# Gated delta stage on one Trainium2 core: fills of the update banks moved, last list through a key bank, norm written in its own order

## The chip, the cores and the metric

The kernel runs on one core of a Trainium2 chip. The metric is the device time of one execution in microseconds (us). The core's engines run their own instruction lists and wait for one another through semaphores: TensorE (PE in the profile, with its weight loads as PEld), VectorE (DVE), ScalarE (ACT), GpSimd (POOL) and SyncE (SP), which issues the DMAs.

## The reference

The program is four layers of attention and feed-forward, each followed by a residual sum and a normalization. The change touches the first one, a gated delta rule, in float32:

```python
q = _causal_dwconv_silu(x @ Wq.T, qcw, qcb)            # 16 heads of 64 channels, 4 taps
k = _causal_dwconv_silu(x @ Wk.T, kcw, kcb) * SCALE
v = _causal_dwconv_silu(x @ Wv.T, vcw, vcb)
a = jax.nn.sigmoid(x @ Wa.T + ba)
beta = jax.nn.sigmoid(x @ Wb.T + bb)

def step(S, inp):
    qt, kt, vt, at, bt = inp
    err = jnp.einsum('bhij,bhj->bhi', S, kt) - vt
    S = at[..., None] * S - bt[..., None, None] * (err[..., None] * kt[:, :, None, :])
    o = jnp.einsum('bhij,bhj->bhi', S, qt)
    return (S, o)

mu = o.mean(-1, keepdims=True)
var = ((o - mu) ** 2).mean(-1, keepdims=True)
o = (o - mu) / jnp.sqrt(var + EPS) * ln_w + ln_b
g = jax.nn.sigmoid(x @ Wg.T)
return (o * g) @ Wo.T
```

The kernel holds 4 sequences of 512 steps, so 4 x 16 heads = 64 states of 64 x 64.

## The kernel before

The stage is `delta_attention`. It takes the 512 steps in 16 passes of 32 (`NC`, index `n`); each pass has two halves of 16 steps (`e` = 0 and 1), and each half two quarters of 8 (`u`). Heads lie in pairs (`NP` = 32) on the 128 partitions.

DVE sets the pace. A half is: `begin` (transposes the start products out of PSUM, L2784), `steps` for the first quarter, the transposed list of values `W` (L2836), `middle` (decays the state `ST`, L2808, then takes what the first quarter gives to the second out of PSUM, L2810), `steps` for the second quarter, `W` again (L2838), and the end of the half: `end` transposes the outputs (L2862) and the next pass's decays and values (L2743, L2744); in the first half `norm` normalizes and gates the outputs of the pass before (L2867, L2870), in the second `gate_keys` transposes the products of keys for the next pass out of PSUM (L2732, L2736). Then `prepare` (L2749, L2752) and the next `begin`.

PE serves this chain. At the end of each half `boundary` updates the state: it turns `W` with 4 transposes (L2476), waits until ACT has copied them to `WT` (L2647, semaphore `wc`), adds 64 small products to the decayed state in four PSUM banks, one bank per row quarter `r` (L2466; `UPDATES` = banks 6, 7, 0, 1), and after ACT has copied each bank back to `ST` (L2659, `state`) makes the start products of the next half (L2442), which DVE's L2784 waits for. The decayed state comes into those banks by a product with the identity, 128 x 512, here called a fill (`kept`, L2447). Between these PE projects the next pass: decays, values, keys, queries (L2381, L2384), into banks 0 and 1 by turns, from where ACT evacuates them (L2593, `evac`). It also makes the products of keys (L2395, 64 of them, into banks 2 to 5), those of the later quarters (L2405), keys across (L2435), centring, gate and variance (L2498, L2502, L2509), the cross products for `middle` (L2416, L2428), and the output projection of the pass before (`out`, L2517).

The order of each engine's work is written out by hand in its `one_pass`. Which bank is free sets most of it. Before the change the lists of the second half were turned in bank 1:

```python
UPDATES = (6, 7, 0, 1)
TURNED = ((2, 3), (1, 1))
EARLY = (4, 3)
```

so in the first half all four banks were filled ahead of `W`, and in the second three; bank 1 was filled after the updates of the other three, and its 16 updates came after that.

Of the kernel before, what the change touches and what calls it, by code (L numbers as in the profile page):

```python
# [15 lines left out]
ALU = mybir.AluOpType  # L16
# [2219 lines left out]
def delta_attention(c):  # L2236
# [7 lines left out]
    M = 8  # L2244
# [4 lines left out]
    NP = B * M  # L2249
# [3 lines left out]
    I = 32  # L2253
    GR, GP = 4, NP // 4
    UPDATES = (6, 7, 0, 1)
    TURNED = ((2, 3), (1, 1))
    EARLY = (4, 3)
    ACROSS = (2, 3)
    BEGUN = 7
    GC = 2 * SB * CP + SB  # L2260
    names = ("loaded", "staged_k", "staged_q", "staged_v", "prepared", "beta_ps", "beta", "proj", "evac", "kq", "g", "gt", "kt", "ktc",
# [3 lines left out]
    s = {n: c.nc.alloc_semaphore(name="dl_" + n) for n in names}  # L2265
    with ExitStack() as ctx:
# [51 lines left out]
        PROJ = 8  # L2318
        K, QQ, V, A = range(4)
        ORDER = (A, A, V, V, K, K, QQ, QQ)  # L2320
        AV = 4
# [49 lines left out]
        def _(eng):  # L2371
            def project(m, first, last, fresh):
                for i in range(first, last):
                    if i - first >= 2 or not fresh:
                        eng.wait_ge(s["evac"], m * PROJ + i - 1)
                    w, half = ORDER[i], i % 2
                    for r in range(4 * half, 4 * half + 4):
                        out = ps[:, i % 2, (r % 4) * P:(r % 4 + 1) * P]
                        cols = slice(r * P, (r + 1) * P)
                        if w == A:  # L2380
                            mm = eng.matmul(out, Wa[:, cols], columns_of(c.X, m, PAD), start=True, stop=True)  # L2381
                        else:
                            for tap in range(TAPS):
                                mm = eng.matmul(out, taps[w][:, tap, cols], columns_of(c.X, m, tap),  # L2384
                                                start=tap == 0, stop=tap == TAPS - 1)
                    mm.then_inc(s["proj"], 1)

            def products_of_keys(m):
                eng.wait_ge(s["kq"], m + 1)
                eng.wait_ge(s["evac"], (m + 1) * PROJ)  # L2390
                eng.sem_inc(c.past, 1)
                for pair in range(NP):
                    for h in range(2):
                        rows, w = slice(DK * h, DK * h + DK), pair % 2
                        mm = eng.matmul(keys_ps[DK * (h ^ w):DK * (h ^ w) + DK, w, pair // 2, :], kkN[rows, pair, :, :].rearrange("p k t -> p (k t)"),  # L2395
                                        kqN[rows, pair, :, :].rearrange("p t k -> p (t k)"), start=True, stop=True)
                mm.then_inc(s["g"], 1)

            def later_products(m):
                for e in range(2):  # L2400
# [45 lines left out]
            def kept(r):  # L2446
                eng.matmul(ps[:, UPDATES[r], :], c.ident[:, :], quarters[:, r, :, :], start=True, stop=False)  # L2447

            def keep_early(n, e):
                eng.wait_ge(s["decayed"], 2 * n + e + 1)  # L2450
                for r in range(EARLY[e]):
                    kept(r)

            def boundary(n, e):
                j4 = 8 * n + 4 * e

                def next_start(r):
                    eng.wait_ge(s["state"], j4 + max(r + 1, 2 * e))
                    eng.sem_inc(c.past, 1)
                    start(1 - e, r)  # L2460

                def update(g, k, h, r):
                    rows, cols = slice(32 * r, 32 * r + 32), slice(DK * h, DK * h + DK)
                    at = (2 * g + k) * DK
                    last = (g, k, h) == (GR - 1, 1, 1)
                    mm = eng.matmul(ps[cols, UPDATES[r], at:at + DK], KT[rows, e, k, g, cols],  # L2466
                                    WT[rows, g, DK * (h ^ k):DK * (h ^ k) + DK], start=False, stop=(g, k) == (GR - 1, 1))
                    if last:
                        mm.then_inc(s["upd"], 1)

                early = EARLY[e]
                eng.wait_ge(s["w"], 4 * n + 2 * e + 2)
                eng.sem_inc(c.past, 1)
                for half in range(2):
                    for g in (2 * half, 2 * half + 1):
                        mm = eng.transpose(ps[:, TURNED[e][half], g * P:(g + 1) * P], W[:, g * GP:(g + 1) * GP, :], c.ident[:, :])  # L2476
                    mm.then_inc(s["t"], 1)
                eng.wait_ge(s["wc"], 6 * n + 3 * e + 3)
                eng.sem_inc(c.past, 1)
                for g, k, h, r in itertools.product(range(GR), range(2), range(2), range(early)):  # L2480
                    update(g, k, h, r)
                for r in range(early, GR):
                    kept(r)
                    for g, k, h in itertools.product(range(GR), range(2), range(2)):
                        update(g, k, h, r)
                for r in range(GR):
                    next_start(r)
                if e == 1:
                    eng.wait_ge(s["gt"], 2 * n + 3)
                    eng.sem_inc(c.past, 1)  # L2490
                    later_products(n + 1)
# [20 lines left out]
            def out(n):  # L2512
                eng.wait_ge(s["normed"], n + 1)
                eng.sem_inc(c.past, 1)
                Dv = Q[:, :].rearrange("p (m x) -> p m x", m=M)
                for m in range(M):
                    mm = eng.matmul(ps[:, 6, 0:P], Wo[:, m, :], Dv[:, m, :], start=m == 0, stop=m == M - 1)  # L2517
                mm.then_inc(s["wo"], 1)

            def one_pass(n, first):  # L2520
                keys_across(n)
                eng.wait_ge(s["ktc"], 5 * n + 1)
                if not first:
                    centre(n - 1)
                project(n + 1, 0, 2, True)
                eng.wait_ge(s["ktc"], 5 * n + 5)
                middle(n, 0)
                if not first:
                    variance(n - 1)
                project(n + 1, 2, AV, False)  # L2530
                eng.wait_ge(s["evac"], (n + 1) * PROJ + AV)
                if not first:
                    eng.wait_ge(s["log"], 2 * n - 1)
                keep_early(n, 0)
                boundary(n, 0)
                project(n + 1, AV, 6, True)
                if not first:
                    out(n - 1)
                project(n + 1, 6, 7, False)
                middle(n, 1)  # L2540
                project(n + 1, 7, PROJ, False)
                if not first:
                    eng.wait_ge(s["scaled"], n)
                    eng.wait_ge(s["wo_copied"], n)
                eng.wait_ge(s["evac"], (n + 1) * PROJ + 7)
                keep_early(n, 1)
                eng.wait_ge(s["begun"], BEGUN * (2 * n + 1) + 5)
                products_of_keys(n + 1)
                boundary(n, 1)
# [11 lines left out]
            project(0, 6, PROJ, False)  # L2561
            eng.wait_ge(s["staged_q"], 32 + 16 * len(late))
            products_of_keys(0)
            eng.wait_ge(s["gt"], 2)
            eng.sem_inc(c.past, 1)
            later_products(0)
# [160 lines left out]
        def _(eng):  # L2727
# [10 lines left out]
            def turn_values(m, e):  # L2738
                span = slice(e * CH, (e + 1) * CH)
                eng.wait_ge(s["evac"], m * PROJ + AV)  # L2740
                if 2 * m + e > 2:
                    eng.wait_ge(s["laid"], 4 * (2 * m + e - 2))
                eng.transpose(decays[:, :, :], aN[:, span, :]).then_inc(s["transposed"], 1)  # L2743
                eng.transpose(values[:, :, :], vN[:, span, :]).then_inc(s["transposed"], 1)  # L2744
# [112 lines left out]
                settled()  # L2857

            def end(n, e, first):
                if e == 0 and not first:  # L2860
                    eng.wait_ge(s["centred"], n)
                eng.transpose(O[:, e * CH:(e + 1) * CH, :], OT.rearrange("p i t -> p t i")).then_inc(s["o"], 1)  # L2862
                turn_values(n + 1, e)

            def norm(n):
                eng.wait_ge(s["log"], 2 * n + 2)
                eng.scalar_tensor_tensor(D[:, :], centred_ps, vec[:, LW:LW + 1], Q[:, :], ALU.mult, ALU.mult).then_inc(s["scaled"], 1)  # L2867
                eng.wait_ge(s["scaled"], n + 1)
                by_row = "p (x m) -> p x m"
                eng.scalar_tensor_tensor(Q[:, :].rearrange("p (m x) -> p x m", m=M), D[:, :].rearrange(by_row, m=M), vec[:, LB:LB + 1],  # L2870
                                         gate[:, :, :].rearrange("p t n -> p (t n)").rearrange(by_row, m=M), ALU.add, ALU.mult)\
                   .then_inc(s["normed"], 1)

            def residual(n):
# [207 lines left out]
```

## Time and profile before

| | |
|---|---|
| time, median of 3 runs | 2895.76 us (2886.55 to 2899.36) |
| the profiled execution | 2886.77 us, span 2885.0 us |
| PE busy | 2413.8 us (84%) |
| DVE busy | 2070.2 us (72%) |
| ACT busy | 1604.8 us (56%) |
| delta stage, about 60 to 1310 us: DVE busy | 1092.4 us |
| the same: PE busy | 1006.6 us |
| the same: mean granted clock of PE | 0.86 |

Times are microseconds from the start of the span. A row of the timeline gives start, duration, engine, line of the kernel, operation, tiles and count; in brackets stands the idle time before it and who ended it. A float32 product leaves two records on PE, a transpose one. The granted clock is 1.00 at 2.4 GHz and 0.50 at 1.2 GHz. A matmul's end is modelled, so where two groups stand back to back the difference of their starts is the better price.

### The profile page before, as it was taken

Reading aid. Unit: us, or ns where it says so; the run is one execution under the profiler, and the core shown is the slowest. Engines: PE = TensorE matmul, PEld = TensorE weight load, DVE = VectorE, ACT = ScalarE, POOL = GpSimd, SP = SyncE. Lnnn points to the kernel's source line nnn. Section 1 sums busy time; section 2 is a strip of 40 time slices with the busy share of each in tenths; the row PEclk is TensorE's granted clock in tenths of the full one; section 3 lists DMA queues with packets and bytes.
Section 4 is the critical chain, followed back from the end, with each engine's and each line's share of the span. In section 5 each row is a group of like instructions: output and inputs, shape, how many; then the busy total and the mean of one; then the engine's idle time right before and its main releaser. Section 6 shows DMA issues by size and latency. Waiting matters only on the chain. (4 is left out here: it accounts for less than half of the span.)

```text
span 2885.0 us, 63703 instructions
## 1 busy us (share of the span) xinstructions
PE 2413.8 (84%) x25649; PEld 1614.8 (56%) x25701; DVE 2070.2 (72%) x3811; ACT 1604.8 (56%) x4104; POOL 260.7 (9%) x278
## 2 busy tenths in 40 slices
PE   6788778887788787788994999999987877998687
PEld 5666667666666666664442666666542322332376
DVE  6888898888888888983113777788626766885365
ACT  3666666666666665665234777777631113776244
POOL 0000000000000000000011101100002432110422
PEclk9888898888888888987996999999998998999889
DMA  5111011111111110102006999999410003220422
GB/s 183 32 32 30 18 31 32 31 32 25 24 31 32 32 32 17 31 17 70 1 11 166 237 250 227 227 248 235 105 37 0 0 0 113 68 68 18 180 58 64
DMA packets 205725, 219.47 MB, mean 76 GB/s; under 512 B 32966, under 2 KB 191446, under 8 KB 199990
## 3 DMA queue, kind: packets, MB, share of 16 engines
q1 hardware_dynamic: 203033, 210.44, 28.0%
q0 software_dynamic: 2400, 4.95, 0.5%
q8 instruction: 206, 3.38, 0.5%
q14 instruction: 86, 0.70, 0.1%
HBM read 137.96 MB, written 79.79 MB: 75 GB/s over the span
## 5 line engine op out<-in xcount | busy, mean ns | idle before, releaser
L2850 DVE TENSOR_REDUCE dl_ZO<-dl_XP 128x64 f32<-128x128 f32 (+6 forms) x448 | 219.8, 491 | 15.4
L1990 ACT ACTIVATE da_AB<-ps 128x384 f32<-128x384 f32 x256 | 124.5, 490 | 139.1 <-PE ps L1851 135.4
L2845 DVE TENSOR_TENSOR dl_XP<-dl_ZO,dl_G 128x128 f32<-128x128 f32 (+5 forms) x384 | 177.1, 461 | 13.2
L2000 ACT ACTIVATE da_E<-ps,da_top 128x512 f32<-128x512 f32 x256 | 176.1, 688 | 17.6 <-DVE da_top L2146 17.2
L1470 DVE TENSOR_REDUCE ra_top<-ps 128x1 f32<-128x512 f32 x256 | 159.3, 681 | 36.0 <-PE ps L1236 22.8
L2143 DVE TENSOR_TENSOR ps<-ps,da_window 128x192 f32<-128x192 f32 (+1 forms) x256 | 101.3, 396 | 115.0 <-PE ps L1874 110.7
L2146 DVE TENSOR_REDUCE da_top<-ps 128x1 f32<-128x512 f32 x256 | 177.0, 691 | 8.8
L1881 PE MATMUL ps<-ident,da_E 128*128 128x128 f32 x1024 | 169.1, 288 | 1.3 <-ACT da_E L2000 1.3
L1370 ACT ACTIVATE ra_PT<-ps 128x512 f32<-128x512 f32 x256 | 135.9, 602 | 61.1 <-PE ps L1267 59.2
L2447 PE MATMUL ps<-dl_ST,ident 128*128 128x512 f32 x256 | 136.1, 667 | 21.5 <-ACT dl_vN L2593 21.5
L1601 POOL MEMSET da_K<- 32x4096 f32 x2 | 7.0, 3506 | 1502.4 <-POOLq L195 1502.3
L2647 ACT ACTIVATE dl_WT<-ps 128x256 f32<-128x256 f32 x64 | 21.1, 381 | 210.9 <-PE ps L2476 210.9
L2384 PEld LDWEIGHTS ps<-X,dl_taps_v 128*128 128x128 f32 x1088 | 128.8, 197 | 14.0 <-issue 9.9
L1881 PEld LDWEIGHTS ps<-ident,da_E 128*128 128x128 f32 x1024 | 108.5, 141 | 50.1 <-issue 39.6
L2384 PE MATMUL ps<-X,dl_taps_v 128*128 128x128 f32 x1088 | 128.5, 279 | 3.7 <-DVE dl_taps_v L2906 3.2
L2384 PE MATMUL ps<-X,dl_taps_k 128*128 128x128 f32 x1088 | 130.3, 280 | 0.2 <-issue 0.2
L2384 PE MATMUL ps<-X,dl_taps_q 128*128 128x128 f32 x1088 | 129.5, 276 | 0.0
L2384 PEld LDWEIGHTS ps<-X,dl_taps_k 128*128 128x128 f32 x1088 | 126.8, 196 | 1.2 <-issue 0.5
L2675 ACT ACTIVATE dl_FB<-dl_F,dl_beta_now 128x32 f32<-128x32 f32 x512 | 126.6, 350 | 0.0
L2384 PEld LDWEIGHTS ps<-X,dl_taps_q 128*128 128x128 f32 x1088 | 125.1, 192 | 1.1
L2833 DVE TENSOR_TENSOR dl_ZO<-dl_ZO,dl_aT 128x64 f32<-128x64 f32 (+5 forms) x384 | 114.9, 299 | 0.0
L2668 ACT ACTIVATE dl_bv<-dl_Wb,dl_beta_now 128x32 f32<-128x32 f32 x512 | 112.9, 334 | 3.2 <-ACT dl_beta_now L2664 0.4
(411 smaller groups left out, 5931.4 us busy)
## 6 DMA issues: line engine op xcount, KB each, us to landing
da_bands<-da_AB SPq DMA_DIRECT2D x128, 384.0 KB, 3.8
dl_Abc<-dl_ends SPq DMA_DIRECT2D x64, 512.0 KB, 6.4
da_window<-da_bands SPq DMA_DIRECT2D x128, 192.0 KB, 4.4
da_across<-da_bands SPq DMA_DIRECT2D x128, 192.0 KB, 4.5
da_parts<-da_split SPq DMA_DIRECT2D x64, 96.0 KB, 3.4
ra_parts<-ra_split SPq DMA_DIRECT2D x16, 384.0 KB, 3.7
rf_We<-in_rf_We SPq DMA_DIRECT2D x1, 4608.0 KB
da_K<-da_parts SPq DMA_DIRECT2D x16, 256.0 KB
```

The source lines that it names most:

```text
L1370: eng.activation(PT[:, k % 2, h, :], ps[:, tscore_bank(UNITS * m + v), :], ACT.Exp).then_inc(s["exps"], 1)
L1470: eng.tensor_reduce(top[:, m % 2, u:u + 1], ps[:, score_bank(UNITS * m + u), :], AXX, ALU.max, negate=True).then_inc(s["maxima"], 1)
L1881: mm = eng.transpose(ps[:, 2 + U % 2, k * P:(k + 1) * P], E[:, U % 2, k * P:(k + 1) * P], c.ident[:, :])
L1990: eng.activation(AB[:, j % STAGES, h, :, :], ps[:, band_bank(v), 0:2 * BAND].rearrange("p (k x) -> p k x", k=2), ACT.Copy)\
L2000: eng.activation(E[:, U % 2, :], ps[:, score_bank(U), :], ACT.Exp, bias=top[:, u:u + 1], accum_out=total[:, m % 2, u:u + 1]).then_inc(s["e ...
L2146: eng.tensor_reduce(top[:, u:u + 1], bank, AXX, ALU.max, negate=True).then_inc(s["maxima"], 1)
L2384: mm = eng.matmul(out, taps[w][:, tap, cols], columns_of(c.X, m, tap), start=tap == 0, stop=tap == TAPS - 1)
L2447: eng.matmul(ps[:, UPDATES[r], :], c.ident[:, :], quarters[:, r, :, :], start=True, stop=False)
L2675: ins = eng.activation(FB[:, e, :, t // SB, t % SB], F[:, e, :, t // SB, t % SB], ACT.Copy, scale=beta_now[:, 1, t:t + 1])
L2833: link(eng.tensor_tensor(mine[:, :, 0:t], mine[:, :, 0:t], aT[:, e, :, u, t + 1].unsqueeze(2).to_broadcast([P, I, t]), ALU.mult))
L2845: link(eng.tensor_tensor(XP[:, :, :, SB - t:], seen.unsqueeze(1).to_broadcast([P, 2, I, t + 1]), G[:, x:x + 2, keys][:, ::-1, :].unsqueeze ...
L2850: link(eng.tensor_reduce(ZO[:, to:to + 1 + (2 * I - 1) * CH:CH].rearrange("p (k i) -> p k i", k=2), XP[:, :, :, SB - 1 - t:], AXX, ALU.add))
```

## The change

It does five things, all in `delta_attention`.

1. The second half's list is turned in bank 4, a bank of the products of keys. The 16 products that write it (`LAST_KEYS`, pairs 1, 3 to 15) are therefore made after the copy of the list and ahead of the updates; the other 48 stay where they were.
2. Bank 1 is filled in both halves between the turning of the list and the wait for its copy; the updates then go over all four banks together.
3. In the first half the fills of banks 6, 7 and 0 stand ahead of the second half of the value projection (which writes bank 1), not behind it. In the second half, two of them no longer wait for the evacuation.
4. `end` turns the next decays and values before the outputs, not after.
5. `norm` writes its result in place in `D`, in the order in which it lies; before it wrote `Q`, rows apart. The output projection reads `D` with a step of 8 elements; before it read `Q` in order.

```diff
-    TURNED = ((2, 3), (1, 1))
-    EARLY = (4, 3)
+    TURNED = ((2, 3), (4, 4))
     ACROSS = (2, 3)
+    LAST_KEYS = range(1, NP // 2, 2)
...
-                for pair in range(NP):
+                key_products(pair for pair in range(NP) if pair not in LAST_KEYS)
+
+            def key_products(pairs):
+                for pair in pairs:
...
-                mm.then_inc(s["g"], 1)
+                return mm
...
                         mm = eng.transpose(ps[:, TURNED[e][half], g * P:(g + 1) * P], W[:, g * GP:(g + 1) * GP, :], c.ident[:, :])
                     mm.then_inc(s["t"], 1)
+                eng.wait_ge(s["evac"], (n + 1) * PROJ + (PROJ if e else AV))
+                kept(3)
                 eng.wait_ge(s["wc"], 6 * n + 3 * e + 3)
                 eng.sem_inc(c.past, 1)
-                for g, k, h, r in itertools.product(range(GR), range(2), range(2), range(early)):
+                if e == 1:
+                    key_products(LAST_KEYS).then_inc(s["g"], 1)
+                for g, k, h, r in itertools.product(range(GR), range(2), range(2), range(GR)):
                     update(g, k, h, r)
-                for r in range(early, GR):
-                    kept(r)
-                    for g, k, h in itertools.product(range(GR), range(2), range(2)):
-                        update(g, k, h, r)
...
-                Dv = Q[:, :].rearrange("p (m x) -> p m x", m=M)
+                Dv = D[:, :].rearrange("p (t m) -> p m t", m=M)
...
-                project(n + 1, 2, AV, False)
-                eng.wait_ge(s["evac"], (n + 1) * PROJ + AV)
+                project(n + 1, 2, 3, False)
                 if not first:
                     eng.wait_ge(s["log"], 2 * n - 1)
-                keep_early(n, 0)
+                eng.wait_ge(s["decayed"], 2 * n + 1)
+                kept(0)
+                kept(1)
+                eng.wait_ge(s["evac"], (n + 1) * PROJ + 3)
+                kept(2)
+                project(n + 1, 3, AV, False)
                 boundary(n, 0)
...
+                eng.wait_ge(s["decayed"], 2 * n + 2)
+                kept(0)
+                kept(1)
                 eng.wait_ge(s["evac"], (n + 1) * PROJ + 7)
-                keep_early(n, 1)
+                kept(2)
...
             def end(n, e, first):
+                turn_values(n + 1, e)
                 if e == 0 and not first:
                     eng.wait_ge(s["centred"], n)
                 eng.transpose(O[:, e * CH:(e + 1) * CH, :], OT.rearrange("p i t -> p t i")).then_inc(s["o"], 1)
-                turn_values(n + 1, e)
...
-                by_row = "p (x m) -> p x m"
-                eng.scalar_tensor_tensor(Q[:, :].rearrange("p (m x) -> p x m", m=M), D[:, :].rearrange(by_row, m=M), vec[:, LB:LB + 1],
-                                         gate[:, :, :].rearrange("p t n -> p (t n)").rearrange(by_row, m=M), ALU.add, ALU.mult)\
+                eng.scalar_tensor_tensor(D[:, :], D[:, :], vec[:, LB:LB + 1], gate[:, :, :].rearrange("p t n -> p (t n)"), ALU.add, ALU.mult)\
                    .then_inc(s["normed"], 1)
```

PE, first half of a pass, around the value projection. Before:

```order
L2509 MATMUL ps<-dl_Q,dl_sums 128x512 x2
L2384 MATMUL ps<-X,dl_taps_v 128x128 x32
L2447 MATMUL ps<-dl_ST,ident 128x512 x4
L2476 MATMUL ps<-ident,dl_W 128x128 x4
L2466 MATMUL ps<-dl_WT,dl_KT 64x64 x64
```

The same place with the change, whose lines have other numbers (L2506, L2450, L2473 and L2464 are L2509, L2447, L2476 and L2466 of before):

```order
L2506 MATMUL ps<-dl_Q,dl_sums 128x512 x2
L2384 MATMUL ps<-X,dl_taps_v 128x128 x16
L2450 MATMUL ps<-dl_ST,ident 128x512 x3
L2384 MATMUL ps<-X,dl_taps_v 128x128 x16
L2473 MATMUL ps<-ident,dl_W 128x128 x4
L2450 MATMUL ps<-dl_ST,ident 128x512
L2464 MATMUL ps<-dl_WT,dl_KT 64x64 x64
```

Three fills have moved ahead of half of the value projection, and one behind the turning of the list.

PE, second half of a pass, from the fills to the start products. Before:

```order
L2447 MATMUL ps<-dl_ST,ident 128x512 x3
L2395 MATMUL ps<-dl_kqN,dl_kkN 64x64 x64
L2476 MATMUL ps<-ident,dl_W 128x128 x4
L2466 MATMUL ps<-dl_WT,dl_KT 64x64 x48
L2447 MATMUL ps<-dl_ST,ident 128x512
L2466 MATMUL ps<-dl_WT,dl_KT 64x64 x16
L2442 MATMUL ps<-dl_kqN,dl_ST 64x32 x64
```

With the change (L2398 is L2395 of before, L2445 is L2442):

```order
L2450 MATMUL ps<-dl_ST,ident 128x512 x3
L2398 MATMUL ps<-dl_kqN,dl_kkN 64x64 x48
L2473 MATMUL ps<-ident,dl_W 128x128 x4
L2450 MATMUL ps<-dl_ST,ident 128x512
L2398 MATMUL ps<-dl_kqN,dl_kkN 64x64 x16
L2464 MATMUL ps<-dl_WT,dl_KT 64x64 x64
L2445 MATMUL ps<-dl_kqN,dl_ST 64x32 x64
```

The fourth fill stands ahead of all updates, 16 products of keys between it and them, and the 16 updates that stood alone have joined the 48.

## Rows read from the trace of the kernel before

**Rows 1.** Waits of DVE, 65 to 1305 us: waiter <- releaser: us, times, longest.

```profile
DVE dl_Y L2784 <- PE ps L2442: 88.9, 31, 4.3
DVE dl_D L2810 <- PE ps L2428: 17.1, 17, 2.0
```

**Rows 2.** Timeline of DVE (start, us, instruction), end of a first half.

```profile
628.13 1.04 DVE L2862 STREAM_TRANSPOSE dl_O<-dl_ZO 128x512 f32<-128x512 f32 x1
...
630.29 1.24 DVE L2867 SCALAR_TENSOR_TENSOR dl_D<-ps,dl_vec,dl_Q 128x1024 f32<-128x1024 f32 x1
...
631.57 2.03 DVE L2870 SCALAR_TENSOR_TENSOR dl_Q<-dl_D,dl_vec,dl_gate 128x1024 f32<-128x1024 f32 x1
...
636.55 1.25 DVE L2784 STREAM_TRANSPOSE dl_Y<-ps 128x1024 f32<-128x1024 f32 x1 [1.54 <-PE ps L2442]
```

**Rows 3.** Timeline of PE in the same half.

```profile
613.67 1.12 PE L2428 MATMUL ps<-dl_GX,dl_WT 64*64 64x64 f32 x16
...
626.26 3.70 PE L2447 MATMUL ps<-dl_ST,ident 128*128 128x512 f32 x8 [1.35 <-ACT dl_vN L2593]
...
631.01 1.58 PE L2466 MATMUL ps<-dl_WT,dl_KT 32*64 32x64 f32 x128 [0.62 <-ACT dl_WT L2647]
```

**Rows 4.** Timeline of ACT in the same half.

```profile
622.74 1.26 ACT L2593 ACTIVATE dl_vN<-ps,dl_vec 128x128 f32<-128x128 f32 x4
...
624.94 1.26 ACT L2593 ACTIVATE dl_vN<-ps,dl_vec 128x128 f32<-128x128 f32 x4 [0.94 <-PE ps L2384]
...
632.59 2.06 ACT L2659 ACTIVATE dl_ST<-ps 128x512 f32<-128x512 f32 x4 [0.67 <-PE ps L2466]
```

**Rows 5.** Timeline of PE in the hashed feed-forward stage.

```profile
2122.98 2.00 PE L347 MATMUL ps<-hf_SH,hf_sw2x 128*128 128x256 f32 x4
2124.80 0.61 PE L344 MATMUL ps<-hf_EH,hf_w 128*128 128x256 f32 x2
```

**Rows 6.** Timeline of PE, the second half of the same pass.

```profile
643.85 1.95 PE L2517 MATMUL ps<-dl_Q,dl_Wo 128*128 128x128 f32 x16
...
645.64 3.74 PE L2384 MATMUL ps<-X,dl_taps_q 128*128 128x128 f32 x32
...
651.42 0.68 PE L2428 MATMUL ps<-dl_GX,dl_WT 64*64 64x64 f32 x16
...
658.38 2.09 PE L2395 MATMUL ps<-dl_kqN,dl_kkN 64*64 64x64 f32 x128
...
665.14 1.08 PE L2476 MATMUL ps<-ident,dl_W 128*128 128x128 f32 x4 [4.66 <-DVE dl_W L2838]
667.06 2.02 PE L2466 MATMUL ps<-dl_WT,dl_KT 32*64 32x64 f32 x96 [0.84 <-ACT dl_WT L2647]
669.01 2.08 PE L2447 MATMUL ps<-dl_ST,ident 128*128 128x512 f32 x2
671.01 1.97 PE L2466 MATMUL ps<-dl_WT,dl_KT 32*64 32x64 f32 x32
672.91 3.64 PE L2442 MATMUL ps<-dl_kqN,dl_ST 64*64 64x32 f32 x128
```

**Rows 7.** Timeline of DVE in that second half.

```profile
652.50 0.71 DVE L2810 STREAM_TRANSPOSE dl_D<-ps 128x512 f32<-128x512 f32 x1
...
667.95 2.27 DVE L2732 STREAM_TRANSPOSE dl_G<-ps 128x2048 f32<-128x2048 f32 x1
...
676.69 1.25 DVE L2784 STREAM_TRANSPOSE dl_Y<-ps 128x1024 f32<-128x1024 f32 x1 [4.29 <-PE ps L2442]
```

**Rows 8.** Timeline of PE at another second half, and the DVE row it releases.

```profile
1143.92 1.09 PE L2476 MATMUL ps<-ident,dl_W 128*128 128x128 f32 x4 [4.33 <-DVE dl_W L2838]
...
1152.89 1.25 DVE L2784 STREAM_TRANSPOSE dl_Y<-ps 128x1024 f32<-128x1024 f32 x1 [1.71 <-PE ps L2442]
```

**Rows 9.** Windows: engines' busy us, granted clock (PEclk), DMA.

```profile
671.00:674.80 3.80, 3.80 (x105) 3.67 (x107) 1.36 (x2) 1.68 (x8) 0.00 (x0) 0.50 0.02 3
...
1149.50:1153.00 3.50, 3.50 (x189) 3.32 (x192) 1.75 (x4) 2.10 (x10) 0.00 (x0) 1.00 0.04 7
```

More of the change, by code:

```diff
@@ L2447, in kept @@
                 eng.matmul(ps[:, UPDATES[r], :], c.ident[:, :], quarters[:, r, :, :], start=True, stop=False)
-            def keep_early(n, e):
-                eng.wait_ge(s["decayed"], 2 * n + e + 1)
-                for r in range(EARLY[e]):
-                    kept(r)
             def boundary(n, e):
@@ L2469, in update @@
                         mm.then_inc(s["upd"], 1)
-                early = EARLY[e]
                 eng.wait_ge(s["w"], 4 * n + 2 * e + 2)
@@ L2477, in boundary @@
                     mm.then_inc(s["t"], 1)
+                eng.wait_ge(s["evac"], (n + 1) * PROJ + (PROJ if e else AV))
+                kept(3)
                 eng.wait_ge(s["wc"], 6 * n + 3 * e + 3)
                 eng.sem_inc(c.past, 1)
-                for g, k, h, r in itertools.product(range(GR), range(2), range(2), range(early)):
+                if e == 1:
+                    key_products(LAST_KEYS).then_inc(s["g"], 1)
+                for g, k, h, r in itertools.product(range(GR), range(2), range(2), range(GR)):
                     update(g, k, h, r)
-                for r in range(early, GR):
-                    kept(r)
-                    for g, k, h in itertools.product(range(GR), range(2), range(2)):
-                        update(g, k, h, r)
                 for r in range(GR):
@@ L2563, in _ @@
             products_of_keys(0)
+            key_products(LAST_KEYS).then_inc(s["g"], 1)
             eng.wait_ge(s["gt"], 2)
```

## The prediction

> **What bounds the kernel now.** I read the stage by windows first: DVE is the busiest engine of it, so what counts is where DVE stands still. Its waits give two places: 88.9 us in 31 waits for the start products, 17.1 us in 17 for the cross products of `middle` [rows 1]. Everything else that the change touches is worth only what it does to these. Then I read one pass (598 to 677 us), each half by the timelines of DVE, PE and ACT. In a first half DVE waits 1.54 us at `begin` [rows 2], in a second half 4.29 us [rows 7]; nearly all second halves are like this one.
>
> The second half's wait is PE's: from the turning of the list at 665.14 PE does turn, 48 updates, fill, 16 updates, start products, one behind the other, until DVE goes on at 676.69, 11.55 us later [rows 6, 7]. In that run the granted clock is 0.50 [rows 9], which is 1.2 GHz; before it PE had stood idle for 4.66 us [rows 6].
>
> **First half, the order of fills and projection.** ACT evacuates the first half of the values from 622.74 to 624.00 and the second from 624.94 to 626.20, and the four fills follow (0.92 us each at 2.4 GHz) [rows 3, 4]. With the change the fill of bank 0 waits for 624.00 and ends near 624.9. The other half of the projection takes 3.6 us (32 records like those of the queries, 3.74 with their tail [rows 6]) and ends near 628.6, its evacuation (1.26 [rows 4]) near 629.9. The fill of bank 1 then runs to 630.85, and the updates begin there, against 631.01: a gain of 0.15 us, no more, although one fill less stands ahead of the list. The price of the new order is on DVE: the decays and values are turned first now and wait for that evacuation, from 628.13 to 629.95, 1.8 us. From the outputs to the ready `begin` DVE has 6.9 us of work (628.13 to 636.55 less 1.54) [rows 2]. The norm becomes shorter: its second step takes 2.03 us, the first, of the same size and in order, 1.24 [rows 2], so 0.8 us. DVE is then ready at 629.95 + 6.9 - 0.8 = 636.05 and PE at 636.4: the new stall is covered with 0.35 us to spare, and the shorter norm is worth nothing by itself.
>
> **Output projection.** Its 16 records take 1.79 us (643.85 to 645.64), 0.112 each for 128 columns read in order [rows 6]. The nearest row of a read with a step of 8 elements is the hashed stage: 4 records of 256 columns in 1.82 us, 0.455 each, where 256 columns in order would be twice 0.112 = 0.224 [rows 5, 6]. So 128 columns cost 0.23 and the projection 3.64 us, 1.85 more; the other bound is 0. PE goes without a gap from this projection through the queries, 645.64 + 3.74 = 649.38, and turns the list only then; the cross products end at 651.42 + 0.68 = 652.10, and DVE takes them at 652.50 without a wait [rows 6, 7], so it has 0.4 us in hand. So 1.45 us of the 1.85 show up as a new wait of DVE in `middle`, in each of 15 passes.
>
> **Second half, the boundary.** From the turning on, with the clock as before: turn 1.06; fill 2.00 (669.01 to 671.01), beside the copy for which PE idled 0.84; 16 products of keys; 64 updates; copies; starts. The keys: 64 took 2.09 us at 2.4 GHz over four quadrants of the array [rows 6], so 16 at 1.2 GHz would be 1.05; but all 16 write one bank from two quadrants only, like the cross products, 16 records in 1.12 us at 1.2 GHz [rows 3], which makes 2.1 for 32 records with the tails and 1.75 without. I take 1.75. Updates: 96 records over three banks took 1.95 [rows 6]; 128 over four take as much if the fourth row quarter runs beside the others, 2.6 if they are issued at the same pace; at 2.4 GHz it was 1.58 [rows 3]. I take 2.0 to 2.6. Ends at 6.8 to 7.4 us after the turning; before it was 7.77 (672.91). But in the kernel before, the copies of three banks were done by then; now all four come due at once. ACT needs 2.06 for four [rows 4]; the first starts need two copies, 1.25 with the latency. Then the starts, 3.64 + 0.14 [rows 6]. Sum 11.85 to 12.4 against 11.55: this boundary **loses** 0.3 to 0.9 us at 1.2 GHz; I take 0.6. DVE gets the keys about 2 us later (670.0 against 667.95), and covers that with its 4.29.
>
> A rule speaks against this place more strongly. The Trainium skill, "TensorEngine Tiling (Array Packing)", section "Gotcha 1: PSUM Pressure", says that different row tiles cannot access the same PSUM bank simultaneously. By it the 32 key records would run one by one, 32 x 0.112 = 3.6 us at 1.2 GHz, and the sum would be 1.8 us a pass worse. The row on the cross products, two row halves into one bank, has 16 records in 1.12 us where one by one they would need 1.8 (0.112 each), so here the trace does not bear the rule out, and I go by the row.
>
> **The clock** decides the rest. One second half of before had the same list of work but rose before the starts: 1.00 from 1149.5 [rows 9], and DVE went on 8.97 us after the turning instead of 11.55 [rows 8]. With the change a rise by then gives: updates done at 6.8, last copy at 9.0, last starts at 9.7, a gain of 1.8. If the clock is still at 2.4 GHz at the boundary, the chain (0.6 + 0.9 + 0.9 + 1.6 + 2.2 + 0.7) is 6.9 us, and DVE's own work to 672.40, 7.26, sets the end: the whole 4.29 goes. Before, PE ran only four transposes between 660.5 and 667.06, and the clock was down every time; now a full-array fill follows the transposes 0.8 us sooner, and each pass has another length, so that the fall meets other work. Per pass, with +1.45 and -0.15: clock as before +1.9; rise before the starts -0.5; never down -3.0. I expect of 15 passes 6, 5 and 4: 11.4 - 2.5 - 12.0 = -3.1. In the first halves the cross products run at 1.2 GHz too (1.12 us [rows 3]) and cost DVE 0.85 a time, of the 17.1 [rows 1]; with other phases I take that away in 5 passes, -4.3. At the stage's end norm and output projection stand in the open: +1.85 - 0.8 = +1.0.
>
> **Sum:** -6 us. The profiled execution (2886.77, span 2885.0) lies 9 below the median; the difference is applied to the median: 2895.76 - 6 = 2890.
>
> **Rivals.**
> 1. *Clock as before in every boundary, strided read in full.* Place: the wait of `middle` in second halves and the copies that no longer overlap. 15 x 1.9 + 1.0 = +30, 2925. It turns slower as soon as more than about 10 of 15 boundaries stay at 1.2 GHz to the starts. For it: in before nearly all did. Against it: the packed work after the list. 0.18.
> 2. *Clock up at almost every boundary.* 12 x -3.0, 3 x -0.5, -4.3, +1.0 = -41, 2855. For it: the fill directly behind the transposes; against it: 4 us of idle before them remain. 0.12.
> 3. *The step of 8 costs nothing.* Then 15 x 1.45 = 22 us less than forecast: 2868. Against it stands [rows 5]; for it, that those reads are 256 wide and of another shape. 0.10.
> 4. *The change does not move the chain*: the four banks gain what the keys and copies cost, and the projection has slack that I miss: 2896. 0.10.
> 5. *The 16 keys run one record at a time* instead of two: 15 x 1.85 us on PE ahead of the updates, where they set the end at either clock level (half at 2.4 GHz). With 6 passes low and 9 high 6 x 1.85 + 9 x 0.9 = +19 on the forecast, 2909. For it: both halves write one bank. Against it: the cross products [rows 3]. It is what the tiling page named above would make of it. 0.04.
>
> **Numbers.** The forecast has 0.46. A measurement of this kernel tells about 0.5%, 14.5 us, from no change: faster means below 2881.3, slower above 2910.2. Faster: rivals 2 and 3 (0.22) and the part of the forecast with more than half of the clock phases on the good side (0.14), 0.36. Slower: rival 1 and half of rival 5, 0.20. Same: the rest, 0.44. The range takes in rival 3 (2868) and goes down almost to rival 2 and up most of the way to rival 1, since both can hold in part: 2858 to 2918.
>
> **What would show it.** Output projection 3.6 us instead of 1.8 and a wait at the cross products of second halves of about 1.5 us (if not, rival 3). The norm's second step near 1.25. DVE waiting about 1.8 us for `vN` before it turns the decays in first halves, and a `begin` wait there near 0. The 16 keys near 1.75 us at 1.2 GHz; near 3.6 would bear out the tiling rule. At `begin` after second halves waits that scatter: about 2.5 to 3 less the later keys at a low clock, near 0 at a high one. I am wrong if these waits are all alike, or if the pass's length falls by more than 2 us.

## The result, and the profile after

The changed kernel takes 2908.52 us (median of 13 runs, 2902.24 to 2919.63) against 2895.76 (13 runs, 2886.55 to 2903.23). The ratio is 1.0049, 95% interval [1.0037, 1.0060]: some 14 us slower, where 6 us faster was forecast. The time lies inside the range, but its sign is the other one.

| | before | after |
|---|---|---|
| the profiled execution, us | 2886.77 | 2910.08 |
| span, us | 2885.0 | 2908.3 |
| PE, DVE, ACT busy, us | 2413.8, 2070.2, 1604.8 | 2416.4, 2064.3, 1599.3 |
| granted clock, whole span | 0.904 | 0.921 |
| granted clock, 60 to 1310 us | 0.86 | 0.90 |

The two profiled executions are 23 us apart, since that of before was 9 below its median; what follows accounts for the 23. PE has 2.6 us more work, DVE and ACT have less, and the clock is higher. The time is in DVE's waits, here over 60 to 1365 us (waiter <- releaser: us in total, times, longest):

```profile
DVE dl_D L2815 <- PE ps L2431: 46.2, 30, 3.1
DVE dl_Y L2748 <- ACT dl_vN L2598: 33.7, 15, 2.8
DVE dl_Y L2789 <- PE ps L2445: 31.5, 24, 3.6
DVE dl_G L2737 <- PE ps L2398: 27.1, 16, 1.9
```

Over the same stretch of the kernel before, the wait at `begin` is 92.9 us ([rows 1], a little shorter, has 88.9). It falls to 31.5 us (now L2789), but 33.7 come up at the values, 27.1 at the keys, and the cross products' go from 17.1 to 46.2. Sum: 110.0 before, 138.5 now.

PE in a second half of the changed kernel, and the DVE rows that wait for it:

```profile
656.61 3.89 PE L2514 MATMUL ps<-dl_D,dl_Wo 128*128 128x128 f32 x16
660.32 3.75 PE L2384 MATMUL ps<-X,dl_taps_q 128*128 128x128 f32 x32
...
679.49 1.09 PE L2473 MATMUL ps<-ident,dl_W 128*128 128x128 f32 x4 [4.33 <-DVE dl_W L2843]
680.37 1.92 PE L2450 MATMUL ps<-dl_ST,ident 128*128 128x512 f32 x2
682.22 1.97 PE L2398 MATMUL ps<-dl_kqN,dl_kkN 64*64 64x64 f32 x32
684.12 1.82 PE L2464 MATMUL ps<-dl_WT,dl_KT 32*64 32x64 f32 x128
687.15 1.32 PE L2445 MATMUL ps<-dl_kqN,dl_ST 64*64 64x32 f32 x74 [1.22 <-ACT dl_ST L2664]
```

```profile
666.84 0.72 DVE L2815 STREAM_TRANSPOSE dl_D<-ps 128x512 f32<-128x512 f32 x1 [1.31 <-PE ps L2431]
...
684.24 2.32 DVE L2737 STREAM_TRANSPOSE dl_G<-ps 128x2048 f32<-128x2048 f32 x1 [1.85 <-PE ps L2398]
...
689.81 1.25 DVE L2789 STREAM_TRANSPOSE dl_Y<-ps 128x1024 f32<-128x1024 f32 x1 [1.08 <-PE ps L2445]
```

The output projection takes 660.32 - 656.61 = 3.71 us where it took 1.79 [rows 6]. The list is turned, bank 1 filled and the keys made without a gap. From the turning to DVE's `begin` it is 10.32 us (11.55 before, [rows 6, 7]). The granted clock there is the third number from the end, 0.50 and then 1.00:

```profile
679.50:684.00 4.50, 4.50 (x38) 3.00 (x38) 2.82 (x5) 1.71 (x3) 0.00 (x0) 0.50 0.00 0
687.20:689.40 2.20, 2.01 (x124) 1.90 (x126) 1.50 (x3) 2.11 (x10) 0.00 (x0) 1.00 0.00 0
```

It is low at the list and up before the starts (taken a microsecond before DVE goes on). That holds for 13 of the 15 second halves behind the first pass; before, it held for one.

For all halves I average the DVE timeline over the 15 passes behind the first. Length is from one `begin` to the next, the other columns are DVE's idle time ahead of that step, all in us:

| | first half: length | cross | values | begin | second half: length | cross | keys | begin |
|---|---|---|---|---|---|---|---|---|
| before | 38.95 | 0.96 | 0 | 1.80 | 40.06 | 0.17 | 0 | 4.03 |
| after | 39.67 | 1.52 | 2.25 | 0.39 | 40.84 | 1.56 | 1.72 | 1.48 |

So the second half loses 0.78 us, which is the strided read less what the boundary gains. The first half loses 0.72 us, and that was not expected.

One thing more stands in PE's rows. In 4 of the 15 second halves PE stops for 1 to 2 us in all between the turning and DVE's `begin`, and the profile names no engine that it waited for ("issue"). One of them:

```profile
1086.48 1.79 PE L2445 MATMUL ps<-dl_kqN,dl_ST 64*64 64x32 f32 x107 [1.22 <-ACT dl_ST L2664]
1090.13 0.48 PE L2445 MATMUL ps<-dl_kqN,dl_ST 64*64 64x32 f32 x19 [1.87 <-issue]
```

These four boundaries take 11.6 to 12.9 us, the other eleven 9.6 to 10.4 (mean 10.06). In the kernel before no boundary of a second half has such a gap. Together the four lie 7.9 us above the others' mean, 0.5 us a pass; in two of them the clock was also low at the starts. Why the gaps fall there no run shows.

### The profile page after: what moved, and what is told of

Same layout as the page of the kernel before. It is cut to its first block and busy times, and to the rows that moved or that the text cites. A ratio compares the mean times of both kernels' runs of the same rounds, so it can differ in the third digit from the quotient of the medians.

```text
span 2908.3 us, 63672 instructions
## 1 busy us (share of the span) xinstructions
PE 2416.4 (83%) x25649; PEld 1607.6 (55%) x25701; DVE 2064.3 (71%) x3811; ACT 1599.3 (55%) x4104; POOL 261.0 (9%) x278
## 5 line engine op out<-in xcount | busy, mean ns | idle before, releaser
L2450 PE MATMUL ps<-dl_ST,ident 128*128 128x512 f32 x256 | 140.3, 663 | 27.8 <-ACT dl_vN L2598 27.8
L2445 PE MATMUL ps<-dl_kqN,dl_ST 64*64 64x32 f32 x4096 | 78.3, 226 | 48.1 <-ACT dl_ST L2664 31.0
```

## The experiments

Each kernel was timed beside the kernel before on the same chip, in three batches: the four `u_` kernels, the next four, the last four. The first batch ran on one chip, the other two on another, so kernels of different batches are compared by their ratios. Between traces only lengths inside the stage are compared: from the last `begin` to the end of the span it is 1572 to 1578 us in the first batch and in the two kernels of this case, 1554 to 1564 in the others. The ratio is not always that of the two medians: the runs of u_second scatter from 2889.94 to 2913.74, and its profiled execution is the slowest of them. Line numbers move by some lines between kernels.

| kernel | what it has of the change | median us | before us | ratio [95%] |
|---|---|---|---|---|
| u_norm | all but part 5 | 2889.34 | 2890.9 | 0.9995 [0.9985, 1.0005] |
| u_first | all but the first half's fills (parts 2 and 3 there) | 2907.52 | 2890.9 | 1.0055 [1.0040, 1.0070] |
| u_second | all but the second boundary | 2907.04 | 2890.9 | 1.0034 [1.0018, 1.0049] |
| u_end | all but part 4 | 2905.62 | 2890.9 | 1.0053 [1.0040, 1.0067] |
| only_norm | part 5 alone | 2896.89 | 2879.24 | 1.0065 [1.0043, 1.0087] |
| second_alone | the second boundary alone | 2872.45 | 2879.24 | 0.9976 [0.9965, 0.9987] |
| fb_before | none; ACT's scalings moved | 2863.51 | 2879.24 | 0.9933 [0.9913, 0.9952] |
| fb_u_norm | as u_norm; scalings moved | 2836.5 | 2879.24 | 0.9852 [0.9837, 0.9868] |
| in_order | all, read without the step (wrong rows) | 2873.16 | 2880.29 | 0.9974 [0.9964, 0.9983] |
| fb_after | all; scalings moved | 2848.31 | 2880.29 | 0.9883 [0.9865, 0.9901] |
| fb_u_norm_end | as fb_u_norm without part 4 | 2838.31 | 2880.29 | 0.9850 [0.9832, 0.9867] |
| fb_second | as second_alone; scalings moved | 2842.32 | 2880.29 | 0.9866 [0.9848, 0.9883] |

### What the strided read costs: u_norm, only_norm, in_order

u_norm takes the change and gives `norm` and the projection back what they had; only_norm makes this edit the other way round in the kernel before:

```diff
-                Dv = D[:, :].rearrange("p (t m) -> p m t", m=M)
+                Dv = Q[:, :].rearrange("p (m x) -> p m x", m=M)
...
-                eng.scalar_tensor_tensor(D[:, :], D[:, :], ...
+                eng.scalar_tensor_tensor(Q[:, :].rearrange("p (m x) -> p x m", m=M), D[:, :].rearrange(by_row, m=M), ...
```

in_order keeps the norm as changed and only takes the step out of the read. Its projection then multiplies rows that belong to other heads and steps, so its output is not the program's; the amount of work is the same:

```diff
-                Dv = D[:, :].rearrange("p (t m) -> p m t", m=M)
+                Dv = D[:, :].rearrange("p (m x) -> p m x", m=M)
```

> The changed kernel with the norm written by rows again and the output projection reading in order. Theory (the strided read is the dearest part): the output projection falls from 3.7 to 1.8 us, DVE's wait for the cross products of second halves from 1.56 on average to about 0.2, 15 x 1.35 = 20 us less; the norm's second step goes back from 1.28 to 2.03 us, which costs up to 0.75 x 15 = 11 us since the first halves have hardly any wait left. Net 9 to 14 us less than the changed kernel, ratio to before 1.000 to 1.002. Rival (the loss sits in the two boundaries, the projection had slack): within 3 us of the changed kernel, ratio 1.004 to 1.006.

> The kernel before with the norm written in its own order and the strided output projection, nothing else of the change. Theory (the strided read is what made the change slower): the projection takes 3.7 us instead of 1.8, DVE waits about 1.3 us for the cross products of second halves, 15 times, and the 0.75 us that the norm's second step saves vanish in the first halves' begin waits of 1.5 to 1.9: 15 to 20 us slower than before, ratio 1.005 to 1.007. Rival (the read costs only because the boundaries use up PE's slack): at most 6 us slower, ratio up to 1.002.

> The changed kernel, but the output projection reads the 128 columns of each of its 8 products in order from the same buffer (so it multiplies the wrong numbers: the rows belong to other heads and steps; the amount of work is the same). It prices the step of 8 by itself, with the shorter norm kept. Theory: projection 1.8 us, the cross products' wait in second halves from 1.56 to 0.1, 15 x 1.4 = 21 us, of which first halves take some back: ratio to before 0.998 to 1.000, the same as or up to 6 us less than u_norm. Rival (the norm's writing matters as much as the read): unlike u_norm by 8 us or more.

DVE's waits in u_norm:

```profile
DVE dl_Y L2748 <- ACT dl_vN L2598: 32.4, 15, 2.8
DVE dl_G L2737 <- PE ps L2398: 26.8, 16, 1.9
DVE dl_Y L2789 <- PE ps L2445: 23.3, 18, 3.5
DVE dl_D L2815 <- PE ps L2431: 23.1, 17, 2.7
```

and in only_norm:

```profile
DVE dl_Y L2784 <- PE ps L2442: 89.8, 32, 5.3
DVE dl_D L2810 <- PE ps L2428: 43.0, 31, 3.4
```

Without the stride the cross products' wait has half its size (46.2 to 23.1, 30 waits to 17); the stride alone brings 43.0 where 17.1 stood. Both gained a little more than I had expected (u_norm 1.000 to 1.002, in_order 0.998 to 1.000). Against the kernel before, taking only the step out turns 1.0049 into 0.9974, 0.75% or 22 us; only_norm alone loses 0.65% [0.43, 0.87]. In_order differs from the changed kernel in nothing but the step, so the read is the cause, and its projection is short again:

```profile
644.22 1.95 PE L2514 MATMUL ps<-dl_D,dl_Wo 128*128 128x128 f32 x16
646.00 3.74 PE L2384 MATMUL ps<-X,dl_taps_q 128*128 128x128 f32 x32
```

In_order is 0.21% below u_norm (across two batches, the intervals just apart): that would be the shorter norm, 6 us, which I had put at nothing.

Where the time of only_norm goes is less simple. Its second halves wait 1.62 us for the cross products (0.17 before), but only 2.58 at `begin` (4.03), and at 40.15 us are no longer than before. What is longer is the first half, 39.71 against 38.95. The shorter wait at `begin` of second halves comes with the clock, which in 11 of the 15 rose before the starts, in the order of before:

```profile
672.44 1.08 PE L2476 MATMUL ps<-ident,dl_W 128*128 128x128 f32 x4 [4.33 <-DVE dl_W L2838]
679.35 2.07 PE L2442 MATMUL ps<-dl_kqN,dl_ST 64*64 64x32 f32 x128
```

```profile
681.56 1.25 DVE L2784 STREAM_TRANSPOSE dl_Y<-ps 128x1024 f32<-128x1024 f32 x1 [1.86 <-PE ps L2442]
```

From the turning to `begin` that is 9.12 us; the 11 take 9.0 to 9.8.

### What the boundary and the orders are worth: u_second, second_alone, u_first, u_end

u_second turns the second half's list in bank 1 again, with bank 1 filled and updated last and all keys made at once. second_alone puts the second boundary of the change into the kernel before (parts 1 and 2 in the second half, with the two fills there that no longer wait) and nothing else. The edit of u_second:

```diff
-    TURNED = ((2, 3), (4, 4))
+    TURNED = ((2, 3), (1, 1))
...
-                if e == 1:
-                    key_products(LAST_KEYS).then_inc(s["g"], 1)
-                for g, k, h, r in itertools.product(range(GR), range(2), range(2), range(GR)):
+                early = 3 if e else GR
+                for g, k, h, r in itertools.product(range(GR), range(2), range(2), range(early)):
                     update(g, k, h, r)
+                for r in range(early, GR):
+                    kept(r)
...
```

> The changed kernel with the second boundary of before: list in bank 1, all keys ahead of it, fill and 16 updates of bank 1 last. Theory: the second boundary is the one part that gains, 4.03 us of begin waits before against 1.48 + 1.72 after, 0.8 x 15 = 12 us; of it 0.5 a pass is lost again in the next first half's wait for the list's copy on ACT, so without it the time rises by 4 to 12 us, ratio 1.006 to 1.009. Rival (ACT takes all of it back, since the four bank copies now come together and its chain starts later): no difference or less time, ratio 1.002 to 1.005.

> The kernel before with the second boundary of the change alone (list in bank 4, fill beside the copy, 16 keys late). Theory: second halves get 0.8 us shorter, first halves 0.3 to 0.6 longer, because ACT reaches the copy of the first list later and DVE waits there: 3 to 8 us less than before, ratio 0.997 to 0.999. Rival A (all of the 0.8 is taken back): 0.9990 to 1.0005. Rival B (it keeps all): 12 us less, 0.996.

u_second's second halves wait as before again (not for the keys, and 3.67 us at `begin` where it was 4.03), yet it is not slower than the changed kernel: its ratio is 0.0015 lower, and the intervals overlap. I had expected a loss of 4 to 12 us; the rival, that the first half takes all of it back, came true (against the changed kernel second halves are 0.39 us longer and first halves 0.39 shorter). The first half's cross products wait 0.94 us in it, as before, and not 1.52. Alone the boundary brings 0.24% [0.13, 0.35], 7 us. In second_alone the second half is 39.29 us (40.06 before), a gain of 0.77; but the first half is 39.57 against 38.95 and gives 0.62 of it back. The traces thus show 2 of the 7 us.

u_first puts the four fills of the first half behind the whole value projection and ahead of the list, u_end turns the outputs ahead of the decays:

```diff
-                project(n + 1, 2, 3, False)
+                project(n + 1, 2, AV, False)
+                eng.wait_ge(s["evac"], (n + 1) * PROJ + AV)
...
-                kept(0)
-                kept(1)
-                eng.wait_ge(s["evac"], (n + 1) * PROJ + 3)
-                kept(2)
-                project(n + 1, 3, AV, False)
+                for r in range(GR):
+                    kept(r)
```

```diff
             def end(n, e, first):
-                turn_values(n + 1, e)
...
                 eng.transpose(O[:, e * CH:(e + 1) * CH, :], OT.rearrange("p i t -> p t i")).then_inc(s["o"], 1)
+                turn_values(n + 1, e)
```

> The changed kernel with the first half's order of before: the whole value projection, then four fills, no fill beside the copy in first halves. Theory (the delayed evacuation costs more than the earlier updates bring): DVE's waits for vN, 33.7 us in 15, vanish, the begin waits of first halves come back to about 1.5 each (from 0.4); net 8 to 15 us less than the changed kernel, ratio 0.9995 to 1.002. Rival (the first half's new order is neutral, as the prediction had it): within 3 us of the changed kernel.

> The changed kernel with the outputs turned before the decays and values. Theory: the outputs' 0.97 us then lie in the wait for vN, 2.25 on average, which falls to about 1.3; in the passes whose first half has no begin wait that is 0.9 us saved, elsewhere less, and ACT's laying of the decays does not limit: 5 to 13 us less than the changed kernel. Rival (the early decays are what lets ACT copy the banks in time): no gain or a loss of some us.

u_first's waits:

```profile
DVE dl_Y L2788 <- PE ps L2445: 59.0, 32, 3.9
DVE dl_D L2814 <- PE ps L2431: 45.9, 30, 2.9
```

Undone, part 3 takes its 33.7 us of waits for the values away and puts 27.5 back at `begin`; the ratio stays (1.0055 against 1.0049). u_end halves the waits for the values (18.2 us) and lengthens those at `begin` (39.0); it stays as well. I had expected 8 to 15 and 5 to 13 us less. Neither order costs or brings anything that these runs can tell; they shift DVE's waits between two lines.

### Who holds up the first half: fb_before, fb_u_norm, fb_after, fb_second, fb_u_norm_end

With the new boundary the first half's cross products waited 1.46 to 1.54 us whichever other part was undone. A pass of the changed kernel where that wait was long, ACT first:

```profile
765.75 0.62 ACT L2664 ACTIVATE dl_ST<-ps 128x512 f32<-128x512 f32 x1
...
766.66 3.53 ACT L2673 ACTIVATE dl_bv<-dl_Wb,dl_beta_now 128x32 f32<-128x32 f32 x16
771.60 1.57 ACT L2612 ACTIVATE dl_GX<-ps,dl_parity 128x256 f32<-128x256 f32 x4 [1.41 <-PE ps L2408]
773.04 3.97 ACT L2680 ACTIVATE dl_FB<-dl_F,dl_beta_now 128x32 f32<-128x32 f32 x16
776.88 2.44 ACT L2619 ACTIVATE dl_KT<-ps,dl_parity 128x512 f32<-128x512 f32 x4
...
781.80 1.98 ACT L2629 ACTIVATE dl_gate<-ps 128x128 f32<-128x128 f32 x8
783.57 0.64 ACT L2647 ACTIVATE dl_WT<-ps 128x512 f32<-128x512 f32 x1
```

then PE and DVE:

```profile
779.98 0.63 PE L2419 MATMUL ps<-ident,dl_W 128*128 128x128 f32 x4 [1.05 <-DVE dl_W L2841]
784.36 1.12 PE L2431 MATMUL ps<-dl_GX,dl_WT 64*64 64x64 f32 x16 [3.75 <-ACT dl_WT L2647]
```

```profile
786.77 0.72 DVE L2815 STREAM_TRANSPOSE dl_D<-ps 128x512 f32<-128x512 f32 x1 [2.86 <-PE ps L2431]
```

PE has turned the list by 780.61 and waits 3.75 us for its copy, because ACT is without a gap from 773.04 on (the rows left out are other copies and a table load of 1.28 us). So the wait that DVE's row gives to PE is in the main ACT's. The edit moves the 16 scalings of `dl_FB` (3.97 us), which only the second half reads, out of this stretch into the next pass's first half, between the two evacuations of the values, where ACT stood idle for 4.79 us:

```diff
@@ ACT, first half
-                eng.wait_ge(s["prep"], 2 * n + 2)
                 middle(n, 0)
...
-                evacuate(n + 1, 2, AV)
+                evacuate(n + 1, 2, 3)
+                if not first:
+                    scale_decays(n, 1)
+                evacuate(n + 1, 3, AV)
+                eng.wait_ge(s["prep"], 2 * n + 2)
                 boundary(n, 0)
...
-                scale_decays(n + 1, 1)
```

(In fb_before and fb_second they stand behind both evacuations.)

> The kernel before with only those 16 scalings moved (there behind both evacuations of values). Theory: in the kernel before ACT was ahead of that copy except in two passes, so 0 to 4 us less, ratio 0.9985 to 1.0. Rival (ACT is short of time in both kernels alike): as much less as fb_u_norm gains on u_norm.

> The changed kernel without its norm, and with the 16 scalings dl_FB of second halves (4.0 us of ACT) moved out of the stretch ahead of the first list's copy into the next pass, between the two evacuations of values, where ACT stands idle for 4.8 us. Theory (ACT's chain behind the four late bank copies is what takes the second boundary's gain back): the first halves' wait for the cross products falls from 1.46 on average to 0.9 or less, 8 us or more off u_norm, ratio to before 0.996 or less. Rival (PE's low clock and order set that wait): the wait stays at 1.4, the ratio at 0.9995.

In fb_before the wait at the cross products falls to 7.2 us, and the first half's part of it from 0.96 to 0.05, with the granted clock there at 0.50 in every pass, as before. PE's wait for the copies of the lists in `middle` (both halves), before and then in fb_before, falls with it, to 32 times 0.78 us:

```profile
PE ps L2428 <- ACT dl_WT L2642: 38.0, 32, 2.9
```

```profile
PE ps L2428 <- ACT dl_WT L2642: 24.9, 32, 0.8
```

The kernel is 0.67% [0.48, 0.87] faster without any part of the change, 19 us by the ratio, where I had said 0 to 4. The two traces do not show these 19 us: first halves are 38.48 us where they were 38.95, but second halves 40.38 where they were 40.06, and DVE's waits at `begin` rise from 92.9 to 103.0 us, as much as those at the cross products fall. The profiled execution of before lies 9 us under its median, that of fb_before 5 over. So the time is measured, and where it was gained in this kernel stays open.

The pair u_norm and fb_u_norm shows it better: first halves 39.79 and 37.70 us, second halves 39.29 and 39.25, that is 32 us over the 15 passes of the 41 between their ratios (expected were 8 or more). The cross products' wait gives 1.44 us of the 2.09 (1.46 to 0.02), the values' 0.59. fb_u_norm, ACT, PE and DVE at a first list:

```profile
600.67 0.60 ACT L2647 ACTIVATE dl_WT<-ps 128x512 f32<-128x512 f32 x1 [2.99 <-PE ps L2419]
...
612.31 3.95 ACT L2680 ACTIVATE dl_FB<-dl_F,dl_beta_now 128x32 f32<-128x32 f32 x16
```

```profile
601.42 2.10 PE L2431 MATMUL ps<-dl_GX,dl_WT 64*64 64x64 f32 x32 [0.78 <-ACT dl_WT L2647]
```

```profile
603.86 0.71 DVE L2817 STREAM_TRANSPOSE dl_D<-ps 128x512 f32<-128x512 f32 x1
```

Now ACT waits for PE, PE waits 0.78 us, from the turning to the end of the copy, and DVE does not wait. In PE's waits for this copy over the stage, that is 32 x 0.78 = 25 us in this kernel and 49.1 in the changed one, first fb_u_norm:

```profile
PE ps L2431 <- ACT dl_WT L2647: 25.2, 32, 1.0
```

then the changed kernel:

```profile
PE ps L2431 <- ACT dl_WT L2647: 49.1, 32, 3.9
```

> The whole changed kernel, norm included, with the 16 scalings moved as in fb_u_norm. Theory: the strided read costs here what it costs there, 15 x 1.4 = 21 us over fb_u_norm less what the norm's 0.75 brings now that first halves are set by DVE (up to 11 us): ratio 0.988 to 0.993. Rival (once ACT is ahead, PE has slack for the read): 0.985 or less.

> The kernel before with the second boundary of the change and the 16 scalings moved behind both evacuations of values; first half, end and norm as before. If the first half's new order (fills ahead of half of the projection) is worth something once ACT is ahead, this is slower than fb_u_norm by 5 us or more, 0.987 to 0.991; if it still only delays the values, it is faster, 0.980 to 0.984.

> fb_u_norm with the outputs turned before the decays and values again. With no begin waits left in first halves (0.06 on average) and a wait for vN of 1.57, turning the outputs in that wait should take 0.9 us off each first half: 10 to 14 us less than fb_u_norm, ratio 0.980 to 0.982. Rival (the early decays are what ACT needs to have the banks copied in time): no gain.

With the scalings moved, the whole change is 1.17% faster than the kernel before, and without the stride 1.48%: fb_u_norm, 0.9852 [0.9837, 0.9868], 43 us below the kernel before, is faster than both kernels of this case. Parts 3 and 4 add nothing to it that these runs can tell (fb_second 0.9866, fb_u_norm_end 0.9850). The scalings alone bring 0.67%, the boundary alone 0.24%, both together (fb_second) 1.34%, more than the sum. fb_after fell in the range I had given; for fb_u_norm_end I had expected another 10 to 14 us, which did not come, and fb_second lies between the two cases that I had set out.

## Why the prediction was wrong

**The output projection: right.** 3.64 us forecast, 3.71 measured; a new wait of 1.45 forecast in second halves, 1.39 measured on average (1.56 - 0.17). 128 columns with a step of 8 elements cost 3.71 / 16 = 0.232 us, 0.112 in order: the hashed stage [rows 5] was the right neighbour, and rival 3 is out.

**The keys: right.** 684.12 - 682.22 = 1.90 us at a granted clock of 0.50, forecast 1.75. One record at a time would have been 3.6 by the prediction's estimate, and rival 5 is out. So these rows do not bear out, for this shape, the rule of the Trainium skill, "TensorEngine Tiling (Array Packing)", section "Gotcha 1: PSUM Pressure", that different row tiles cannot access the same PSUM bank simultaneously. That DVE gets the keys later is true too (1.72 us a pass), and was covered.

**The first half's stall at the values: right.** 1.8 us forecast and 2.25 measured, with `begin` at 0.39 where near 0 was said. Parts 3 and 4 do nothing, as forecast (-0.15 us).

**The second boundary: its gain comes from the clock, as said, but the size is wrong.** The updates were to end 6.8 us behind the turning and ended at 6.45. But the step "last starts at 9.7" put 0.7 us between the last copy and DVE. It is 689.81 - 687.99 = 1.82, ACT's copies running from 685.93 for 2.06. [Rows 2, 4] had it already: 636.55 - 634.65 = 1.90 at the high clock. So a boundary in which the clock rises takes 10.3 us (mean of the 13, two with the gap marked "issue" among them) and gains 1.2 us on one of before that stays low, and not 1.8. With the clock risen the new order itself gains nothing: where it rises in the order of before, the boundary takes 8.97 us [rows 8], and 9.0 to 9.8 in only_norm (mean 9.2). The worse step is the clock's three cases. I gave "never down" 4 passes of 15 at -4.3 us; it came in none, and in the pass shown PE still stands idle ahead of the list (4.33 us at 679.49). "Rise before the starts" came in 13, not 5; in the other two the clock was low at the starts. The boundaries' term was 6 x 0.6 - 5 x 1.8 - 4 x 4.3 = -23 us; it was -9 (second halves +0.78, less 1.39 for the read, 15 times) to -12 (by u_norm's second half, 39.29 us).

**The first half's cross products: wrong in kind.** "In the first halves the cross products run at 1.2 GHz too ... and cost DVE 0.85 a time ...; with other phases I take that away in 5 passes, -4.3." The low clock alone does not make this wait: fb_before has it at 0.05 us with the same low clock. It is ACT's copy of the first list, behind two series of scalings, the copies of the keys, and the gate. I had read ACT only around the values and the state [rows 4], not in this stretch. And it moved against the change. ACT needs the same time from the last state copy to the list's copy (median 16.7 us before and after), while DVE now starts its quarter 1.8 us (median) behind that state copy, not 3.06, and so arrives at the list earlier against ACT. The wait grew by 0.56 us, and the first half as a whole by 0.72: +11 us where -6.5 was forecast (with the -0.15). What the second half gains by an earlier start, the first half returns: second_alone shows the same without stride and orders. It need not be the new boundary that brings the start forward. In only_norm it comes with the risen clock (1.5 us behind the copy), and there too the first half is 0.76 us longer, 0.26 of it at the cross products.

**The sum**, 15 passes, in us of the profiled pair: the read +21 (forecast +22), the boundary -9 (forecast -23), first halves +11 (forecast -6.5): +23 against -6. Of the 29 between them 14 are the boundary's (the clock's cases and the distance behind the last copy) and 17 the first half's, less 2 at the other terms. Rival 1 gave the right side, 2925 with the read in full, but its mechanism, a clock that stays low to the starts, did not hold: the clock rose in 13 of 15. That the time lies in the range says little, for the range is 60 us wide.

Open stays: why the first half in the changed kernel is 0.72 us longer while its cross wait explains 0.56 (the profile of before is 9 us from its median, more than the rest); the 0.21% put down to the shorter norm, which no kernel isolated within one batch; what makes the clock rise, since it did so in 8 to 14 of 15 second halves in all kernels with the new boundary, but also in 11 in only_norm, against 1 in before and fb_before and 4 in u_second; the gaps marked "issue"; and where fb_before gains its 19 us, of which its trace shows 2.

## What to carry to other kernels

Follow a wait one releaser further before pricing it. DVE's row named PE, PE's own row named ACT, and ACT's timeline showed 4 us of work ahead of the copy that nobody needed until half a pass later. When a chain of several engines is shortened at one place, ask which other chain starts at the same event and does not become shorter, for that one sets the end next. And a read order that saves VectorE 0.75 us but doubles a float32 product on TensorE is paid by whoever waits behind that product.

## What was not expected of the hardware

- The granted clock rose before the start products in 13 of 15 second halves, against one before; yet at the list it was low or partly low (0.50 to 0.75) every time, as before. The new order is not needed for it: the strided read alone brought 11 of 15 (only_norm). The whole rise of the stage's mean, 0.86 to 0.90, bought less than the read took.
- Two row halves of the array writing one PSUM bank did 32 records in 1.90 us at 1.2 GHz, 0.059 each, even a little faster than the cross products' 16 in 1.12 (0.070) [rows 3] from which they were priced.
- Behind the last copy of the state it took 1.8 to 1.9 us until DVE could take the start products at 2.4 GHz, in the two boundaries read above, though by the program only the last 16 of the 64 products wait for that copy.
- PE stood still for 1 to 2 us, with no engine named, inside 4 of the 15 second boundaries of the changed kernel and inside none of the kernel before.
